# Moved stages of a two-layer transformer kernel: output products, spikes, layer norms, projection and tail at other places of the order

## The reference, cut to what matters

```
h  = layernorm(x)
# layer 0, attention: 16 heads, three attentions (causal with latent keys, 64 selected rows, causal with plain keys),
#   each softmax(q k^T / sqrt(96)) v, mixed by a gate softmax(mean_t(h @ w_gate))
x1 = x + attention0(h) @ w_proj
# layer 0, spiking FFN
hid = square(relu(layernorm(x1) @ W_fc.T)); y = hid @ W_proj.T
mem = 0;  5 times: reset = mem > 1; mem = 0.9*mem + y - reset; spikes += (mem > 1)
x2 = x1 + spikes / 5
# layer 1, attention: 16 heads of 16, rotary q and k, causal
x3 = x2 + softmax(q k^T / 4) v @ W_o.T         with q, k, v from layernorm(x2) @ W_qkv.T
# layer 1, FFN
out = x3 + layernorm(x3) @ sign(weight).T
```

## Time and profile before

| | |
|---|---|
| median of 3 runs | 3486.68 us (3484.27 to 3486.93) |
| the profiled execution, its own time | 3490.49 us |
| its span (first to last instruction) | 3488.8 us |
| mean granted TensorE clock in it | 0.941 |
| PE busy, PEld, DVE, ACT, POOL | 92%, 66%, 57%, 43%, 26% |
| DMA queues, share of 16 engines' time | 4.7% and 0.3% and 0.3% |
| PE in the chain that ended last | 71% of the span |

### The profile page before, as it was taken

How to read it: one execution, slowest core, us unless ns; L and a number is a source line. 1 busy time by engine, 2 the same in 40 slices (tenths; PEclk the granted TensorE clock), 3 DMA queues, 4 the chain that set the end, 5 groups by cost and what they waited for, 6 DMA issues and landing times.

```text
span 3488.8 us, 58151 instructions
## 1 busy us (share of the span) xinstructions
PE 3200.9 (92%) x20368; PEld 2317.8 (66%) x20368; DVE 1993.9 (57%) x6929; ACT 1503.5 (43%) x3340; POOL 915.8 (26%) x1828
## 2 busy tenths in 40 slices
PE   4999999899998999989999899998999989999888
PEld 3776776667766677665776667766677666776655
DVE  4665556556565655656556565565555655555445
ACT  1554343453344544435444354443544434444334
POOL 0222222222232222222223222232222322222231
PEclk7999999999998999989999899998999989999899
DMA  3000000000000000000000000000000000000000
GB/s 106 19 19 13 19 13 19 13 7 19 13 19 13 7 19 19 14 12 7 19 19 19 7 7 19 25 13 7 13 19 19 13 1 17 15 19 1 1 1 13
DMA packets 34287, 55.97 MB, mean 16 GB/s; under 512 B 3536, under 2 KB 16592, under 8 KB 33744
## 3 DMA queue, kind: packets, MB, share of 16 engines
q1 hardware_dynamic: 34000, 52.26, 4.7%
HBM read 48.06 MB, written 4.19 MB: 15 GB/s over the span
## 4 chain that ended last, share of the span: by engine, by line
PE 71%; DVE 10%; issue 3%; POOL 3%; ACT 3%; DVEq 0%; ACTq 0%; POOLq 0%
PE outs L1003 14%; PE work L922 7%; PE work L878 5%; PE work L959 4%; PE work L960 4%; PE work L961 4%; PE work L899 4%; PE work L1010 4%; PE work L1028 3%; PE work L1039 3%; PE work L769 3%; PE work L963 2%; PE work L874 2%; PE work L1048 2%; DVE work L1226 1%
## 5 line engine op out<-in xcount | busy, mean ns | idle before, releaser
L1598 ACT ACTIVATE PR<-work 128x512 f32<-128x512 f32 (+1 forms) x1088 | 639.9, 598 | 743.2 <-PE work L961 650.7
L1226 DVE CUSTOM_DVE_ANT_0 work<-work,KEEPB 128x128 f32<-128x128 f32 (+3 forms) x1536 | 668.8, 480 | 234.2 <-PE work L922 234.1
L1717 POOL TENSOR_SCALAR_AFFINE_SELECT PR<-PR 128x256 f32<-128x256 f32 (+1 forms) x960 | 344.4, 366 | 679.9 <-ACT PR L1598 674.1
L1207 DVE TENSOR_TENSOR BIG<-work,BIG 96x512 fp32r<-96x512 f32 (+1 forms) x448 | 279.7, 628 | 381.3 <-ACT BIG L1492 380.5
L922 PE MATMUL work<-BIG 96*128 96x448 f32 (+8 forms) x1664 | 462.9, 368 | 33.4 <-DVE NMX L1226 11.8
L1003 PE MATMUL outs<-PR,ONES 128*32 128x512 f32 (+4 forms) x2304 | 423.6, 476 | 0.0
L959 PE MATMUL work<-BIG 99*128 99x512 f32 (+4 forms) x1152 | 418.6, 363 | 2.6 <-DVE NRM L1259 1.3
L1707 POOL TENSOR_TENSOR TOK<-AB 128x256 f32<-128x256 f32 (+1 forms) x320 | 215.7, 675 | 773.0 <-DVE AB L1177 738.6
L922 PEld LDWEIGHTS work<-BIG 96*128 96x128 f32 (+1 forms) x1664 | 277.1, 197 | 186.9 <-issue 89.8
L960 PE MATMUL work<-BIG 96*128 96x512 f32 (+4 forms) x1152 | 393.3, 341 | 0.0
L961 PE MATMUL work<-BIG 96*128 96x512 f32 (+4 forms) x1152 | 391.4, 340 | 0.0
(11 more groups left out here) (167 smaller groups left out, 5278.5 us busy)
## 6 DMA issues: line engine op xcount, KB each, us to landing
WKW<-w_kw_dram SPq DMA_DIRECT2D x64, 256.0 KB, 2.6
WSEL<-w_sel_dram SPq DMA_DIRECT2D x64, 256.0 KB, 3.0
HN<-x_dram SPq DMA_DIRECT2D x8, 512.0 KB, 3.9
X<-x_dram SPq DMA_DIRECT2D x8, 512.0 KB, 3.8
out_dram<-X SPq DMA_DIRECT2D x7, 512.0 KB, 2.9
WFC<-w_fc_dram SPq DMA_DIRECT2D x1, 1024.0 KB, 9.5
WFP<-w_ffp_dram SPq DMA_DIRECT2D x1, 1024.0 KB, 11.4
WQKV<-w_qkv_dram SPq DMA_DIRECT2D x1, 768.0 KB, 12.7
```

The source lines that it names most:

```text
L1207: read_work(v.tensor_tensor(dst[1], src, dst[0].bitcast(F32), ALU.subtract), use)
L1226: last = v.tensor_tensor_reduce(ps[:, lo:hi], ps[:, lo:hi], KEEPB[:, T - (hi - lo):T], -1.0, -NEG, ALU.add, ALU.min, dst)
L1598: a.activation(PR[0:rows, j % NP, :], ps[0:rows, :], ACT.Exp).then_inc(exp_ready, 1)
L1717: gp.affine_select(blocks, blocks, [[0, len(cols)], [1, P]], ALU.is_ge, 0.0, base=0, channel_multiplier=-1).then_inc(exp_masked, 1)
```

## The change

The tables of due times are replaced, several steps are split, and some buffers are changed.

- `PROJ`: the projection of sample n leaves the start of the layer-1 pass and stands at the end of the layer-0 pass of the same sample, in every layer-0 pass. `proj_early` sums groups 0 to 2 into two held banks, `proj_last` adds group 3. The adds and the variances are steps of their own.
- `MID_A`: `ln` 1, `hT` 1 and the first four `fc` of sample n stand at the end of the layer-1 pass between its two layer-0 passes. `MID_B`: `y` in four quarters (`q`), from position 8.85 on (before: two halves from 17.5), the second from 36.11 (before 39); spikes in six steps `k` = 0 to 5 and the variances as a seventh, from 20.13 and 44.02 (before, one step each at 23.5 and 45). The bank of `y` is held from the first quarter to `k` = 4.
- `TAIL`: twelve steps in place of seven, from -11.69 to 6.51; it uses HN0 for rows and OT for the transposed rows. Banks 0 and 1 stay held until the adds. The wait for `kr_ready` in the tail goes.
- Sample 7 uses HN and HT as the others do.
- x goes into HN0 after the store of the tail (`load_rows(n + 3)`), the second sample's after `pro` 11 of sample 1.
- `PRO`: `pro` 0 at 59.74 (62.0), `pro` 9 at 89.51 (90.0), `pro_pe` 4 at 93.51 (91.5), `pro_pe` 5 at 96.19 (93.5). `AFTER` and `HEADS` change by tenths, `v` 0 to 102.51 (104.0).

Number and size of the instructions stay as they were. The diff, cut to its core:

```diff
+TAIL = [[("wo", 0, -11.69), ("wo", 1, -11.36), ("tail_add", 0, -11.27), ("tail_add", 1, -6.4),
+         ("tail_var", 0, -3.0), ("tail_var", 1, -2.5), ("tail_ln", 0, 0.5), ("tail_ln", 1, 1.56),
+         ("hT", 3, 0, 2.56), ("hT", 3, 1, 3.47), ("sign", 0, 4.51), ("sign", 1, 6.51)],
...
+MID_A = [[("ln", 1, 0, -9.61), ("ln", 1, 1, -7.83), ("hT", 1, 0, -7.49), ("hT", 1, 1, -6.19), ("fc", 0, 0, -5.19),
+          ("fc", 0, 1, -4.53), ("fc", 0, 2, -3.63), ("fc", 0, 3, -3.14)],
+         [("ln", 1, 0, 36.02), ("ln", 1, 1, 37.77), ("hT", 1, 0, 39.08), ("hT", 1, 1, 39.58), ("fc", 0, 0, 40.01),
+          ("fc", 0, 1, 40.89), ("fc", 0, 2, 42.42), ("fc", 0, 3, 46.04)]]
+MID_B = [("y", 0, 0, 8.85), ("y", 0, 1, 10.0), ("y", 0, 2, 11.26), ("y", 0, 3, 12.5), ("spike", 0, 0, 20.13),
...
+         ("spike", 0, 5, 22.69), ("var", 2, 0, 23.52), ("y", 1, 0, 36.11), ("y", 1, 1, 37.47), ("y", 1, 2, 40.0),
+         ("y", 1, 3, 40.63), ("spike", 1, 0, 44.02), ("spike", 1, 1, 45.14), ("spike", 1, 2, 46.31),
...
+PROJ = [("proj_early", 98.19), ("proj_last", 101.97), ("proj_add", 0, 102.07), ("proj_add", 1, 103.03),
+        ("var", 1, 0, 103.32), ("var", 1, 1, 103.48)]
...
-        else:
-            add(PROJ[0], 0)
+        add(PROJ, s)
...
+        if s == 1:
+            add(MID_A[0], 0)
         if s:
-            add(MID[0], s - 1)
+            add(MID_B, s - 1)
...
-        if s < B - 1:
-            add(PROJ[1], s + 1)
+        if s < B - 2:
+            add(MID_A[1], s + 1)
         if s == B - 2:
-            add(MID[1], B - 1)
+            add(MID_C, B - 1)
...
-            elif what in ("proj", "hT", "fc", "v"):
+            elif what in ("hT", "fc", "v", "sign"):
                 work.use(x)
+            elif what == "proj_early":
+                for i in range(2):
+                    work.hold(("proj", n, i))
+            elif what == "proj_add":
+                work.held.discard(work.of["proj", n, x[2]][0])
+            elif what == "tail_add":
+                work.held.discard(x[2])
             elif what == "y" and x[3] == 0:
                 work.hold(("y", n, x[2]))
-            elif what == "spikes":
+            elif what == "spike" and x[3] == 4:
                 work.held.discard(work.of["y", n, x[2]][0])
...
-                    elif x[0] == "tail" and x[2] == 3:
+                    elif x[0] == "sign" and x[2]:
                         store(n)
+                        if n + 3 < B:
+                            load_rows(n + 3)
...
-            def project(n, i):
-
-                ps, done = take(("proj", n, i), W)
+            def project_early(n):
+
+                for i in range(2):
+                    ps, _ = take(("proj", n, i), W)
+                    for g in range(NG - 1):
+                        was_read(pe, work, work_read, (n, 0, "group", g))
+                        add_group(ps, i, g, WP)
+
+            def project_last(n):
                 was_read(pe, work, work_read, (n, 0, "group", NG - 1))
-                for g in range(NG):
-                    last = add_group(ps, i, g, WP)
-                last.then_inc(done, 1)
+                for i in range(2):
+                    k = work.of["proj", n, i][0]
+                    add_group(WB[k], i, NG - 1, WP).then_inc(work_full[k], 1)
...
-            def second_products(n, i, tt):
-                use = ("y", n, i)
-                ps = take(use, W)[0] if tt == 0 else WB[work.of[use][0]]
-                for f in range(NF):
+            def second_products(n, i, q):
+                use, tt = ("y", n, i), q // 2
+                ps = take(use, W)[0] if q == 0 else WB[work.of[use][0]]
+                for f in range(NF // 2 * (q % 2), NF // 2 * (q % 2 + 1)):
...
+            def spikes(n, i, k):
...
+                if k == 0:
+                    ps = full(dve, use, WORK)
...
+                    then(v.tensor_scalar(total, ps[:, :], THRESHOLDS[0], None, ALU.is_ge))
+                elif k < 5:
+                    ins = v.scalar_tensor_tensor(total, WB[work.of[use][0]][:, :], THRESHOLDS[k], total, ALU.is_ge, ALU.add)
...
+                elif what == "tail_ln":
+                    normalised_rows(3, powers(3, n, x[2]), x2(n), HN0, 2 * x[2], 2)
...
-                        half_out(x, x[3], ht(x[1]))
+                        half_out(x, x[3], OT[:, 0:NC, :] if x[2] == 3 else HT)
```

More of the change, by code:

```diff
@@ L319, in end_kept @@
     def end_kept(self, name, k):
-        self.held.discard(k)
         self.take(name, k, 1)
@@ L1129, in _ @@
                 attention(*z)
-            for j in range(4):
-                tail(B - 1, j)
+            for x in TAIL_LAST:
+                tail(x)
         @block.vector
```

317 lines of the change are left out of this document (156 added, 161 removed).

## The result

| | before | after |
|---|---|---|
| median, four runs each on one chip | 3486.8 us (3484.3 to 3486.9) | 3220.1 us (3219.7 to 3220.7) |
| ratio, 95% interval | | 0.924 (0.922 to 0.925) |
| the profiled execution, its span | 3490.5, 3488.8 us | 3220.1, 3218.3 us |
| PE busy in it | 3200.9 us | 3080.5 us |
| PE idle in it (span less busy) | 287.9 us | 137.8 us |

The direction and the places were right, the size was not. The first split of the 270.5 us of span is the subtraction in the table: TensorE is idle for 150.1 us less, and busy for 120.4 us less, with the same 20368 instructions. The forecast had 91 and 35 for these two.

A forecast was written before the change was run, and what follows sets the result against it. TensorE, busy for 92% of the span, was taken as the bound: its work, its gaps and a lower clock. The terms summed to -126 us; 3490.5 less 126 and 3.8 gave 3362 us, 8-in-10 range 3290 to 3450.

The forecast's parts named there:

- 1, projection: End of layer-0 pass: projection fills the wait for POOL's group-3 sum, VectorE's maxima take some back; -35 us.
- 2, tail: Start of layer-0 pass: tail's adds and variances move behind maxima, half of the gap stays; -15 us.
- 3, mask: Product for the positions: moved behind two more units, TensorE's wait for the mask goes; -17 us.
- 4, spikes: Spikes in six steps: TensorE's waits behind VectorE's 5.5 us block go; -28 us.
- 5, norm of x: Layer norm of x: POOL's power step moves ahead, half of the masks' 2.98 us wait goes; -10 us.
- 6, first rows: First layer norm's rows leave the first pair's pieces, -4 us; last sample's spikes, -3; moving first hidden units, 0.
- 7, clock: TensorE's lower clock after three removed waits: half of its cost comes back; -35 us, bounds -74 and 0.
- 8, banks: Work banks held longer by y and `proj_early` cost waiting room: +3 us a sample, +21 us.
- The end waits only move: Rival, pass boundaries: VectorE is already slower there, so projection, tail and norm of x give nothing; 3427 us, chance 0.25.
- Too few banks: Rival, ring of work banks: each added position with a held bank costs a wait, slower; 3514 us, chance 0.10.
- the whole gap goes: Rival, TensorE's gaps: projection and tail reach their bounds, mask and spikes count in full; 3276 us, chance 0.17.

The follow-up runs named there:

- e1: Changed kernel with the projection, its adds and variances back at the start of the layer-1 pass (samples 1 to 7): 3254.5 us.
- e2: Changed kernel with the tail back at its old due times at the start of the layer-0 pass, new buffers kept: 3236.8 us.
- e4: Changed kernel with the last mask steps and the products for positions and selected rows back at old due times: 3265.1 us.
- b3: Kernel before with one part added: spikes in six steps and variances as a seventh, from the old positions: 3439.4 us.
- e3: Changed kernel with the six spike steps and the variance in one block again, at 23.5 and 45.0: 3305.7 us.
- b4: Kernel before with spikes in steps, mask and position steps at new due times, and layer norm of x at 59.74: 3359.1 us.
- e6: Changed kernel with the layer norm of x back at 62.0, behind layer 1's last queries and keys, which move forward: 3268.5 us.
- e5: Changed kernel with first layer norm, transposes, first four hidden-unit steps, first output products and their spikes back in the layer-0 pass: 3261.3 us.
- e8: Changed kernel with both the tail and the first half of the hidden units back at their old places: 3254.3 us.
- b1: Kernel before with idle TensorE products, results unused, in front of four kinds of wait; no step moved: 3408.0 us.
- e7: Changed kernel with the banks of y held 10.1 and 8.5 positions longer, no instruction moved: 3249.2 us.

## Why the prediction was right in kind and wrong in size

Term by term, the idle time first, since it can be read from the two traces. Rows 1 and 2 multiply the one stretch shown by the number of samples; the others are sums over the whole span:

| part | forecast, us | idle time, trace | run |
|---|---|---|---|
| 1, projection | -35 | 7 x (10.4 - 3.8) = -46 | e1: 34 |
| 2, tail | -15 | 6 x (4.8 - 2.1) = -16 | e2: 17 |
| 3, mask | -17 | 24.7 to 7.9 = -17 | e4: 45 with its clock |
| 4, spikes, and 3 of part 6 | -31 | 34.8 to 2.3 = -32 | b3: 42, e3: 86 |
| 5, norm of x | -10 | all waits at POOL's masks: 34.8 to 1.1 = -34 | b4: 12 of the wait; e6: 48, of another wait |
| 6, first rows | -4 | 11.1 to 1.2 = -10 | e5, and e8 less e2: 41 and 17 |
| 7, clock | -35 | busy time: -120 | b1: 108 by the clock alone |
| 8, banks | +21 | rest of the sum: +5 | e7: 0.21 us a position |

The idle rows give -155, and the rest to -150 is +5 for all that was added. (Row 6 takes the waits of the pieces' transposes for ACT, 5.9 to 1.2, and of the middle's transposes for the low parts, 5.2 to 0, both from the waits view.)

**Parts 1 to 4 held.** Four waits of different kinds were read from the timeline, priced, and found gone, within 4 us in parts 2 to 4 and 11 in part 1. In part 1 both halves of the account erred a little: the work filled the gap as said, and VectorE took 1.7 us back instead of 5.5.

**"I take half" in part 5 held for its own wait; the waits around it had no term.** In b4, where the norm moves and the queries and keys of layer 1 next to it do not, the wait of 2.98 us becomes 1.27, so 1.7 us a sample or 12 in all go, beside the 10 that were forecast. In the whole change this wait goes completely, and so do the small ones at the same masks, another 34.8 - 7 x 2.98 = 13.9 us. The full list of waits had one line with 34.8 us in 30 times for them; the part worked from a single entry of the timeline.

**"I take half, as new short waits will pull it down elsewhere" in part 7 failed, and it is the largest miss.** 85 of the 144 us by which the sum was off are here. The estimate of a low microsecond (0.44 us) was right: 0.43 and 0.46 in two kernels. Its count was not. The part counted 23.9 low us a sample, those behind three of the waits (22.1 of them TensorE was busy), and halved them. It left out the two pass boundaries, though the earlier trace rows has their clock: 0.91 of 37.5 us and 0.77 of 22.3 us are 6.8 and 10.3 us at the lower level, 17 a sample. It also left out the 3.4 us behind the first spikes (1319.1 to 1322.5, clock 0.53). And the new waits pulled little down: 277 us went, 40 a sample, and the changed kernel keeps about 10 a sample, 3.4 behind the wait of 1.68 us and 6.9 behind that of 1.58. Even the bound of -74 was too narrow. The Trainium skill, "TensorE: Matmul & The Clock Gate", Part 1, puts the ramp penalty under 1% of a typical span, in a paragraph on the first matmuls of a kernel. As a bound for this kernel, where the lower level comes back several times a sample, it fails: b1 wins 74 us through this term, 2% of the time.

**Part 6 put the move of the first half at nothing**, because TensorE's work is uncovered in either place. That looked at one engine. The move takes VectorE's rows out of the first units of the pass, which is what lets the tail go there (e5 and e8).

**Part 8 was right in price.** If 0.21 us holds for the 12.4 positions too, it is 7 x 12.4 x 0.21 = 18 us against 21. But the waits view names no wait for such a bank, and only 5 us of idle time are not accounted for, so the first positions may cost less than the added ones of e7. The two banks that `proj_early` holds were not tested. (The added positions are 12.3, not 12.4, which changes nothing.)

**The rivals.** "The end waits only move" is out: e1 and e2 cost what parts 1 and 2 said. "Too few banks" is out by e7. The nearest was "the whole gap goes" with 3276, 56 us above what was measured; even every part at its own best bound, -59 - 29 - 17 - 28 - 20 - 7 - 74 = -234, gives 3253, 33 us too slow. The bounds of part 7 above all were too near, and the waits around part 5 had none.

The single undos add up to 34 + 17 + 86 + 45 + 41 + 48 = 271 us, beside 267 gained. That the two are so close is partly luck: e3 overstates its part by about 40 us and e5 by 24, and the moves that nothing undid (heads, values, quarters of y, and what removed 27 us at POOL's masks beyond b4) would have to fill that. Which of those moves freed POOL's masks was not tried and stays open.

## What to carry to other kernels

Price a gap on TensorE with the low-clock stretch that stands behind it, counted from the trace for every gap that the change closes, and when a change closes most gaps, don't halve that term: here the stretch was worth as much as the gap (22 us of waiting and 24 of slower work for the mask). Read each kind of wait from the list over the whole span, not from one entry of a timeline. And where work is moved, look at what leaves the queue of the second engine as well as of the first: a move that is worth nothing to TensorE can be what makes room for the next one.

## What the runs showed of the chip that was not expected

- Products that do nothing pay. 360 of them, 95.3 us of TensorE, took 235 us of the lower level away and made the kernel 74 us faster, although no work was removed. A microsecond at the lower level cost 0.43 us between before and after and 0.46 us between before and b1, beside the 0.44 of the earlier trace rows.
- The stretch behind a gap is not a constant. In e4 the same wait of 2.09 us was followed by 13.7, 10.2, 17.0 and then 3.4 us at the lower level, with TensorE busy throughout; in the kernel before, a wait of 2.41 us was followed by 13.6. So one stretch can't be multiplied by the number of samples.
- Nor is the price of a low microsecond the same everywhere. By the same working e1 has 176 - 135 = 41 us more at the lower level than the changed kernel and e2 has 20, but TensorE is busy for only 4.5 and 2.3 us more. Why they come so cheap is not shown.
- What is left of the lower level in the changed kernel has the same form. The stretches view of the changed kernel behind the 1.58 us wait at the start of a pass:

```profile
1146.40:1153.30 6.90, 6.90 (x19) 5.23 (x18) 6.80 (x39) 0.00 (x0) 0.00 (x0) 0.51 0.01 2
```
